# Reordering the third unit's gating, splitting and copies, and the first scores' sums, in a one-core gated cross-attention and sparse feed-forward kernel

## The reference, cut to what matters

```python
# x, ctx: (32, 128, 512) float32; mask: (32, 128); g_xattn, g_ffn: (1,); w_gate, w_up: (512, 2048); w_down: (2048, 512)
def attention(h, ctx, mask):
    scores = einsum('bsd,bmd->bsm', h, ctx) / sqrt(512)
    attn = softmax(where(mask[:, None, :], scores, -1e30))
    return einsum('bsm,bmd->bsd', attn, ctx)          # zero where no key is valid

def ffn(x):
    h = silu(x @ w_gate) * (x @ w_up)
    # of each group of 4 neighbouring columns of h the 2 of largest magnitude are kept
    return sparsify_2to4(h) @ w_down

x = x + tanh(g_xattn) * attention(layernorm(x), ctx, mask)
x = x + tanh(g_ffn) * ffn(layernorm(x))
```

## Time and profile before

| | |
|---|---|
| median of 3 runs | 1080.91 us (1080.62 to 1082.78) |
| profiled execution | 1081.23 us, span of its instructions 1079.4 us |
| TensorE busy | 1069.8 us, 99% of the span |
| VectorE busy | 795.1 us, 74% |
| ScalarE busy | 611.6 us, 57% |
| GpSimd busy | 225.8 us, 21% |
| DMA | 252.67 MB, mean 234 GB/s |

### The profile page before, as it was taken

The page is one execution under the profiler, slowest core; times in us unless marked ns, Lnnn a source line. Parts: engine busy times, 40 slices in busy tenths (PEclk is TensorE's granted clock), DMA queues, the critical chain, the costliest instruction groups (busy, mean ns, idle before and its releaser), DMA issues.

```text
span 1079.4 us, 15220 instructions
## 1 busy us (share of the span) xinstructions
PE 1069.8 (99%) x5000; PEld 881.5 (82%) x5000; DVE 795.1 (74%) x1389; ACT 611.6 (57%) x1126; POOL 225.8 (21%) x343
## 2 busy tenths in 40 slices
PE   8999999999999999999999999999999999999998
PEld 7888877888888888888888888888888888888887
DVE  6999889998987676677757576676866464665756
ACT  7999786777755454444544454444544444443452
POOL 6888411211111111110001111111000111111121
PEclk9999999999999999999999999999999999999999
DMA  9998986999899777888799777888797667676726
GB/s 315 319 315 292 384 332 151 341 315 303 269 280 363 169 198 185 217 233 240 204 298 281 185 182 205 202 222 243 202 331 221 155 154 189 153 191 152 205 25 144
DMA packets 89822, 252.67 MB, mean 234 GB/s; under 512 B 9104, under 2 KB 9872, under 8 KB 85648
## 3 DMA queue, kind: packets, MB, share of 16 engines
q1 hardware_dynamic: 68144, 203.45, 54.1%
q0 software_dynamic: 21600, 48.24, 26.6%
HBM read 153.09 MB, written 98.57 MB: 233 GB/s over the span
## 4 chain that ended last, share of the span: by engine, by line
PE 92%; DMA 2%; DVE 2%; issue 2%; ACT 1%; SPq 0%; POOL 0%; ACTq 0%; DVEq 0%; POOLq 0%
PE ps_y L1431 11%; PE ps_y L1429 11%; PE ps_y L1430 11%; PE ps_a L1335 10%; PE ps_a L1333 10%; PE ps_a L1337 10%; PE ps_d L1333 5%; PE ps_d L1337 5%; PE ps_d L1335 5%; PE ps_y L1397 3%; PE ps_c L1360 2%; PE ps_c L1337 2%; PE ps_c L1335 2%; PE ps_c L1333 2%; PE ps_a L1352 1%
## 5 line engine op out<-in xcount | busy, mean ns | idle before, releaser
L634 POOL DMA_DIRECT2D out_rows<-y_out x124 | 105.6, 852 | 705.9 <-ACT y_out L786 702.9
L786 ACT ACTIVATE y_out<-ps_y,ffn_gate 128x512 f32<-128x512 f32 x124 | 85.4, 689 | 241.2 <-PE ps_y L1431 241.2
L1333 PE MATMUL ps_a<-xm,w_ring 128*128 128x512 f32 x512 | 199.8, 390 | 0.5 <-DVE hidden L1056 0.5
L1335 PE MATMUL ps_a<-xm,w_ring 128*128 128x512 f32 x512 | 199.6, 390 | 0.0
L1337 PE MATMUL ps_a<-xm,w_ring 128*128 128x512 f32 x512 | 199.5, 390 | 0.0
L1431 PE MATMUL ps_y<-dn,h_lo 128*128 128x512 f32 x480 | 187.2, 390 | 0.0
L1429 PE MATMUL ps_y<-dn,h_hi 128*128 128x512 f32 x480 | 187.1, 390 | 0.0
L1430 PE MATMUL ps_y<-dn,h_hi 128*128 128x512 f32 x480 | 186.7, 389 | 0.0
L1070 DVE TENSOR_TENSOR beats<-h_abs 128x512 bf16<-128x512 f32 x186 | 117.8, 686 | 1.3 <-ACT h_abs L756 1.3
L1333 PEld LDWEIGHTS ps_a<-xm,w_ring 128*128 128x128 f32 x512 | 96.1, 188 | 21.4 <-issue 1.0
L1337 PEld LDWEIGHTS ps_a<-xm,w_ring 128*128 128x128 f32 x512 | 96.1, 188 | 20.2
(11 more groups left out here) (124 smaller groups left out, 1875.6 us busy)
## 6 DMA issues: line engine op xcount, KB each, us to landing
w_ring<-w_scratch SPq DMA_DIRECT2D x147, 512.0 KB, 4.4
out_rows<-y_out POOLq DMA_DIRECT2D x124, 256.0 KB, 4.1
w_scratch<-w_ring SPq DMA_DIRECT2D x56, 512.0 KB, 6.6
xm_scratch<-x_out SPq DMA_DIRECT2D x40, 512.0 KB, 5.8
xm<-xm_scratch SPq DMA_DIRECT2D x19, 1024.0 KB, 10.0
w_raw<-in_L_ffn_w_down SPq DMA_DIRECT2D x9, 1024.0 KB, 7.4
x_in<-in_x SPq DMA_DIRECT2D x32, 256.0 KB, 4.9
ctx_in<-in_ctx SPq DMA_DIRECT2D x32, 256.0 KB, 5.2
```

Of the source, the lines that this page charges most:

```text
L634: nc.gpsimd.dma_start(out[RING * (n // (2 * TILES * QS)) + TILES * ORDER[order] + n % TILES], y_out[:, n % 4], accum_op=ALU.add).then_inc( ...
L786: nc.scalar.activation(y_out[:, n % 4], ps_y[n % 2][:], ACT.Identity, scale=ffn_gate[:]).then_inc(y_copied, 1)
L1333: nc.tensor.matmul(to, w_ring[:, k, e, 0, c], xm[:, k, 0, c], start=begins and c == 0, stop=False, skip_group_check=not begins)
L1335: nc.tensor.matmul(to, w_ring[:, k, e, 0, c], xm[:, k, 1, c], start=False, stop=False, skip_group_check=not begins)
```

## The change

- Third unit: two tiles of h are thinned and split first and the copies of d0 follow them, on ScalarE and VectorE; the other two tiles come behind. On VectorE the five compares go ahead of w_low(2,4), the count of wins ahead of w_low(2,5), and `x_low_at(0, 1)` and both `add_c11` go behind the c22 sums.
- `gated0(1, 0)` goes between `w_sum(2, 2)` and `w_sum(2, 3)`.
- In steps 6, 10 and 14 the x part goes behind copy_d0 (ScalarE) and behind add_c22 (VectorE).
- Attention: block 0's scores are scaled and reduced in slot 2 instead of 3; the mask's first part is loaded after block 1; the third group of six idle transposes is gone.

```diff
-IDLE_TURNS = (12, 10, 6)
+IDLE_TURNS = (12, 10)
@@ SP
-                if b == 2:
+                if b == 1:
                     load_mask(0)
@@ ScalarE, s == 1
                         copy_a1(u, 0)
                         copy_a1(u, 1)
-                        for j in tiles:
+                        for j in tiles[:2]:
                             h_high(0, 0, j)
                         copy_d0(u, 0)
                         copy_d0(u, 1)
+                        for j in tiles[2:]:
+                            h_high(0, 0, j)
@@ ScalarE, s > 1
                         copy_a1(u, 0)
                         copy_a1(u, 1)
-                        x_high_at(s, 0)
+                        if s < QS or s % QS != 2:
+                            x_high_at(s, 0)
                         copy_d0(u, 0)
                         copy_d0(u, 1)
+                        if s > QS and s % QS == 2:
+                            x_high_at(s, 0)
@@ VectorE, attention
-                b = n - 3
-                if 0 <= b < B:
+                b = 0 if n == 2 else n - 3
+                if 0 <= b < B and n != 3:
                     wait(dve, probs_done, b - 1)
                     dve.wait_ge(scores_done, b + 1)
@@ VectorE, s > 1
-                    if s > QS:
+                    if s > QS and s % QS != 2:
                         x_low_at(s, 0)
                     add_c22(u, 0)
                     add_c22(u, 1)
+                    if s > QS and s % QS == 2:
+                        x_low_at(s, 0)
@@ VectorE, s == 1
-                    w_low(dve, nc.vector, 2, 6)
-                    add_c11(2, 0)
-                    add_c11(2, 1)
                     for j in tiles[:2]:
                         h_low(0, 0, j)
+                    keep(0, 0, tiles[2:])
+                    w_low(dve, nc.vector, 2, 6)
                     add_c22(u, 0)
                     add_c22(u, 1)
                     for j in tiles[2:]:
                         h_low(0, 0, j)
+                    add_c11(2, 0)
+                    add_c11(2, 1)
+                    x_low_at(0, 1)
                     compare(0, 1, first + second)
                     compare(0, 1, REST)
@@ VectorE, s == 0
                     w_sum(dve, 2, 2)
+                    gated0(1, 0)
                     w_sum(dve, 2, 3)
-                    gated0(1, 0)
                     gated0(1, 1)
                     w_low(dve, nc.vector, 2, 2)
                     gated1(1, 0)
                     gated1(1, 1)
                     w_low(dve, nc.vector, 2, 3)
-                    x_low_at(0, 1)
+                    compare(0, 0, REST + second)
                     w_low(dve, nc.vector, 2, 4)
+                    count_wins(0, 0)
                     w_low(dve, nc.vector, 2, 5)
-                    compare(0, 0, REST + second)
-                    count_wins(0, 0)
-                    keep(0, 0, kept_order(0))
+                    keep(0, 0, kept_order(0)[:2])
@@ TensorE
             score(0)
-            idle_turns(IDLE_TURNS[2])
             turn_x(1)
```

## The result

| | before | after |
|---|---|---|
| median, same chip, 17 runs each | 1081.07 us (1080.05 to 1082.78) | 1083.24 us (1082.46 to 1084.35) |
| profiled execution, and its span | 1081.23, 1079.4 | 1082.73, 1080.9 |

The ratio is 1.0014, 95% interval 1.0007 to 1.0020; the two medians lie a little further apart, 2.2 us. The ratio is inside the 0.2% that was called no change, though the median is 0.1 above the 1083.1 that stood for it. The time is inside the wide range of 1078.8 to 1083.5, but only by 0.26 us; it is 2 us above the forecast of 1081.2 and 1 us above the forecast's own range of 1080.3 to 1082.2. By the interval the change costs 0.8 to 2.2 us, where the sum of the forecast had +0.25.

The account below looks back on a forecast made before the run. TensorE was 92% of the last-ending chain, with VectorE's queue the later at 197.33. Third unit +1.1, steps -0.60 and start -0.25 made +0.25 us: 1081.2 us, own range 1080.3 to 1082.2, wide range 1078.8 to 1083.5.

Parts of the forecast that it names:

- The start: Up to the first transposed probabilities at 13.89: the start's edits gain 0.25 us, bounds -0.66 to +0.3.
- a clock lost in the start: Rival, 9.5 to 13.6 us: TensorE's clock falls without idle transposes, 1.3 to 2.5 us lost, 1082.5 to 1083.7; chance 0.09.
- Two queues, the small stop at 197.33 decides: Unit 3's product 5: TensorE's and VectorE's queues meet, VectorE's later; removing earlier TensorE stops gains nothing unless VectorE's shortens.
- The gated product: TensorE's stop at 150.86: gated0(1,0) ready by 150.1, so the stop goes, -0.69 us at this place.
- spread(3,1) behind w_low(2,5): Third unit: ScalarE's spread waits until w_low(2,5) runs at 160.5, 2.3 us later, delaying a1's copies and h's high parts.
- The new stops: TensorE at unit 2's product 4, y's fourth tile, unit 3's first product and product 5: 1.2, 1.9, 0.8, 0.35 us.
- The count of twenty low parts: ScalarE's spread(3,1) waits for 7*2 + 6 = 20 low parts, and the twentieth is w_low(2,5).
- Steps 6 and 10: Copy of d0 ahead of x's part: TensorE's stop at step 6 goes, -0.60 us; step 10 gives nothing back.
- The mask's share of the 3.5 us: Start, between x of blocks 2 and 3: mask takes 1.8, ctx 2 and x 3 0.85 each; block 2's x at 8.8.
- The idle transposes: Six in the start, between first scores and turn_x(1), took 0.66 us; what hangs on turn_x(1) could come 0.66 earlier.
- Moved stores: Rival, after 170: w_scratch stores meet w_raw loads, ScalarE waits, VectorE passes it on; +1 to +2 us, chance 0.09.
- the first rival: Removed stops after the attention stay recovered: 1076.1 to 1076.8 us, or 1078.8 if half does; chance 0.12.

Follow-up runs that it names:

- t1_third: Kernel before with only the gated product moved and the third unit's new order: 1082.17 us against 1081.92, ratio 1.0006.
- t6_low5_first: t1_third with w_low(2,5) back ahead of the counting of wins: 1080.81 us; before 1081.98, ratio 0.9992.
- t10_low5_plus: t6_low5_first with two more compares on VectorE in unit 2's second half, results unread: 1081.54 us; before 1081.90, ratio 1.0001.
- t5_dve_plus: Kernel before with two more compares on VectorE in unit 2's second half, results unread: 1082.02 us against 1081.98, ratio 1.0004.
- t4_gate: Kernel before with only gated0(1,0) moved ahead of w_sum(2,3): 1082.00 us against 1081.92, ratio 1.0001.
- t3_late_x: Kernel before with only the x parts of steps 6, 10 and 14 moved behind the copies of d0: 1081.60 us against 1081.92, ratio 0.9998.
- t7_mask_early: Kernel before with only the mask's first part loaded after block 1 instead of block 2: 1082.85 us against 1081.98, ratio 1.0010.
- t9_after_mask_back: The changed kernel with the mask's load back behind block 2: 1081.44 us; before 1081.90, ratio 0.9999.
- t2_start: Kernel before with only the start's three edits (early mask load, third idle transposes out, block 0's scores in slot 2): 1083.39 us against 1081.92, ratio 1.0018.
- t8_no_idle_turns: Kernel before with only the third group of six idle transposes removed: 1081.76 us against 1081.98, ratio 0.9997.
- t11_repaired: Before with gated product's move, third unit as in t6_low5_first, steps as in t3_late_x, no third idle transposes: 1080.74 us against 1081.90, ratio 0.9992.
- t12_repaired_scores: t11_repaired with block 0's scores in slot 2: 1080.08 us; before 1081.90, ratio 0.9990.

## Why the prediction was right, and where it was wrong

**The total: inside the wide range by luck.** The forecast was +0.25 with an own range of -0.6 to +1.3; measured is +1.5 by the ratio and +2.2 by the medians. The start alone was off by 1.6 us. The wide range reached up to 1083.5 for the sake of a clock lost in the start, and no run shows that; the mask's load filled the room that was left for it.

**Two queues, the small stop at 197.33 decides: right, and shown** for this order with full clock. With the clock down behind 167 TensorE's queue is the later one at 197, and 58 of 99 executions of before had less than full clock; the prediction had only the other case. Taking 3.2 us of stops away brought nothing (t1_third); making VectorE's queue shorter by removing one wait brought 1.36 (t6_low5_first). Making it longer is shown less well: in t10_low5_plus +1.20 in five executions with full clock and +0.73 in all, in t5_dve_plus nothing, since there TensorE is the later queue in most executions.

**The gated product: right.** Gone at 150.86 and returned later (t4_gate), in after as forecast.

**spread(3,1) behind w_low(2,5): right.** Forecast at 160.5, with 2.3 idle; measured 161.66 with 2.23 idle, of which 0.85 is the lateness that the start had brought (t1_third, without it: 160.74). The new stops were forecast at 1.2, 1.9, 0.8 and 0.35 and are 1.08, 1.75, 0.73 and 0.49; VectorE's wait for h's high part at 1.5, measured 1.54. The sum was forecast at +1.1; +0.77 in t1_third's and in after's profile, and 1.2 in t1_third's median against before's executions with full clock. The prediction's rows gave 170.4 less 169.4, so 1.0, and the tenths that it names would have made it less; it took 1.1. The count of twenty low parts, read in the code, carried all of this.

**Steps 6 and 10: right.** -0.60 forecast, -0.64 in the profile of after, -0.65 in t3_late_x's; t3_late_x's median alone would not show it. As steps 10 and 14 show no difference, nothing came back.

**The start: wrong, in sign and in two terms.**
- *The mask's share of the 3.5 us.* I gave the mask 1.8 and ctx 2 and x 3 0.85 each, so x of block 2 was to land at 8.8. It landed at 9.59 in after and 9.77 in t7_mask_early: after against t9_after_mask_back (7.33) and t7_mask_early against before (7.00), the mask's 128 KB put it back by 2.3 to 2.8 us. With 9.6 as the bound that I had given +0.3, the size at 14 us came out at +0.6 in after and +0.8 in t7_mask_early. Splitting a sum of three unlike loads by guess was the error; nothing in the trace spoke for the middle.
- *The end of the effect.* I priced the start by the one matmul at 13.89 and stopped there. VectorE and GpSimd were also later (the mask's conversion by 2.0, VectorE's statistics of block 4 by 1.9), and VectorE, 29.35 of 30 us busy, can't catch up until the attention ends. TensorE is covered until 106 us; then 0.70 more is lost in after, 0.75 in t2_start, 0.89 in t7_mask_early, and 0.0 in t9_after_mask_back. That is the reasoning of the third unit, which I made there and left out here. The start comes to +1.36 in all in the profile, where I had -0.25. The medians agree in size: +1.5 in t2_start, and 1.6 to 1.8 come back in t9_after_mask_back.
- *The idle transposes* cost about what was said, 0.5 of the 0.66 in one profile and 0.2 in the median, inside its interval.
- *Not settled:* the mask's load alone costs 0.9 in the median and the idle transposes gave back 0.2, yet the three edits together cost 1.5. The rest would be the early scores, which wait 1.21 us for a late mask in after and hold up the statistics behind them; they were not tried alone with the early mask, the intervals of the three kernels are as wide as this rest, and in the profiles it is t7_mask_early that is later at 122 us (1.79 against 1.14).

**TensorE's clock: the rival had the right mechanism in the wrong place.** It was looked for at 10 to 13 us, where the longest pauses are 1.1 to 1.7 us, and no profile has a fall there. It falls behind the long stop at 167 in four profiles, and 58 of 99 executions of before had less than full clock; I took the one profile, in which it didn't, for all. The Trainium skill, page "TensorE: Matmul & The Clock Gate", Part 1, says that an idle stretch brings the lower clock back; t4_gate's windows agree, with 0.50 after 2.8 us idle. Its price by the medians of before is 1.1 us (1082.14 less 1081.08). The change removes that stop: after's longest is 1.6 idle, and 14 of its 17 executions had full clock. In the later groups this wins something back: t1_third is 0.25 above before's median and 1.2 above its executions with full clock. In the result above it hardly shows. Before's 17 runs there have a median of 1081.07, that of executions with full clock; their clocks are not on record. Against the 99 later runs of before, median 1081.95, after's 1083.24 would be 1.3 above and not 2.2.

**Moved stores: TensorE loses nothing by them.** From unit 3's product 5 to step 6 it stays 2.13 to 2.18 late in after. ScalarE waits at 185.4 for a weight block:

```profile
187.94 1.68 ACT L345 ACTIVATE w_ring<-w_blk 128x512 fp32r<-128x512 f32 x3 [2.55 <-DVE w_blk L362]
```

This is the wait of 1.44 in the earlier trace rows, now 2.55 and 2.1 us later, still for VectorE's sums and not for a store. Ahead of 207.55 it waits 2.15 for a load of w_raw, where before waits 1.62 ahead of 204.87. Of the other kernels with unit 2's and 3's work as in before, t8_no_idle_turns waits 3.17 there and t7_mask_early 1.38, so this wait is not a mark of the moved stores.

**Sum by what was measured:** third unit +0.8 to +1.2, steps -0.6, start +1.36 make +1.6 to +2.0 against an execution of before with full clock. 1081.08, the median of the 41 such, plus that is 1082.7 to 1083.1, beside 1083.11 for after's 14 executions with full clock and 1083.24 for all.

One slip has no effect: in the first rival 3.2 + 0.3 + 0.6 + 0.25 is 4.35, not 4.1, so its time is 1076.1 to 1076.6.

## What to carry to other kernels

Before a stop is removed, look for the engine without idle time that meets TensorE next; only the later queue sets the end, and an edit is worth what it does to that one. See in more than one execution which queue that is: here a fall of the clock turned it round. Carry an edit's effect on every engine's queue to the next place where they meet, even a hundred microseconds on, and not only to the first matmul. In a row of waits on counts, find out which instruction makes the count full: moving one low part behind 2.7 us of other work cost 1.4 us, where the best kernel here wins 1.8.

## What the runs showed of the hardware that I had not expected

- A stop of 2.3 to 2.8 us idle can bring the granted clock to 0.50, the 1.2 GHz level, for about 3 us, though not each time: the profile of before has 2.29 idle and full clock, t7_mask_early 2.42 and full clock, t2_start 2.3 and 0.50. In the runs of t1_third, t6_low5_first and t9_after_mask_back, with no stop above 1.6 after the start, none of 33 executions had a mean clock below 1.000; in before 58 of 99 had. After, t11_repaired and t12_repaired_scores had some (6 of 39) with no such stop in their profiles, which stays open. The times of before so come in two groups about 1.1 us apart, and one profile shows only one of them.
- A load of 128 KB for the mask, read in rows of 1 KB into every partition, pushed the load behind it back by 2.3 to 2.8 us: x of block 2 is there at 9.38 to 9.77 in the three profiles with the early mask, and at 7.00 to 7.61 in ten of the other eleven (8.49 in t1_third). Why it takes so long, and whether it could stand later still, was not tried.
- The first twelve transposes start 0.21 us apart, the 1.2 GHz level, in all 14 profiles. The step to 0.11 came anywhere from 4.4 us (t2_start) to 7.6 (t1_third). With an unchanged start the stretch at 13.89 began anywhere from 13.86 to 14.33, and late beginnings mostly go with a late step (14.27 and 14.33 with 7.6), but 13.86 goes with 6.7 and 13.89 with 4.8, so that the one is not shown to come from the other. This scatter is as large as the edits of the start, and a single profile can't price them.
